# Shift rows transposed in the first place of their slot, and projections read once from the turn bank: four stages of attention on one core

## The chip, the cores and the metric

The kernel runs on one core of a Trainium2 chip. Its time is the device time of one execution in microseconds (us), and of several runs the median counts. The engines are named as in the profile: PE is TensorE's matmuls and PEld its weight loads, DVE is VectorE, ACT is ScalarE, POOL is GpSimd, and SP is SyncE, which issues most DMA transfers. ACTq is ScalarE's own queue of DMA issues.

## What is computed

Sixteen sequences of 512 tokens and 256 features go through four residual layers, each on the layer norm of its input: causal attention, a guided attention that splits the tokens into two classes, rotary attention, and the guided attention again. All have 16 heads of 16 features. From the reference, shortened:

```python
x = x + _L0_attn_a_ref(_layernorm(x), Wq, bq, Wk, bk, Wv, bv, Wo, bo)      # causal
x = x + _L0_ffn_ref(_layernorm(x), g_info, W_qkv, W_proj, b_proj)          # guided
x = x + _L0_attn_b_ref(_layernorm(x), Wqkv, Wo)                            # rotary
x = x + _L0_ffn_ref(_layernorm(x), g_info, W_qkv, W_proj, b_proj)          # guided
...
# guided: the class of a token is its mean cosine with g_info, scaled to 0..1 over all tokens, > 0.9
logits = jnp.einsum('bqhd,bkhd->bhqk', q * scale, k)
l = jnp.where(key_mask[:, None, None, :], logits, -jnp.inf)
a = jax.nn.softmax(l, axis=-1)
```

## The kernel before

**Stages and batches.** The four layers are the stages 0 to 3: `STAGES = [CAUSAL, SPLIT, ROTARY, SPLIT]`. A stage runs over 16 batches, one sequence each. While a batch of a stage is in attention, the batch before it is finished (output projection, residual, layer norm, and the projections q, k and v of the next stage, called `nx`, `nq`, `nv`). In stage 0 the projections of later batches of its own (`xt`, `qk`, `v`) come on top. The classes of a guided stage need all of its tokens, so there is a full stop ahead of stages 1 and 3; stage 2 follows stage 1 without one.

**Precision.** q and k are each split into three bf16 parts (`parts`: high, middle, low), which go out to memory and come back as stacked rows of `q_stack` and `k_stack`, so that one bf16 matmul over 96 to 100 rows gives the exact scores.

**Slots.** A batch has 16 slots. In slot n, TensorE does in this order: four matmuls of `scores_t` (keys on the partitions; L1235), of which ScalarE takes the exponential into `probs` (L1072); score tiles 0 and 1 of the head six slots ahead (L1204), of which VectorE takes the maximum (L874); the turn of the first place; the output sums `o_ps` (L1256); tiles 2 and 3; the turn of the second place. The two banks of the score tiles alternate, so a tile waits for the maximum two tiles back. There are four heads to a group, and a group g starts its `scores_t` in slot 4g.

**The shift.** When the 16 maxima of a group are there, VectorE writes their negative as two bf16 parts into `shift_parts` (a cast, L884, and a subtraction, L886; semaphore `shift_ready`). The turn `sh` transposes them on TensorE (L1302), VectorE copies them to `shift_rows` (L924), and ScalarE's queue issues the transfer into two rows of `q_stack` (L1092). `scores_t` of the group waits for it (`shift_in`). The maxima of groups 1, 2 and 3 are complete at the end of slots 1, 5 and 9, and those of the next batch's group 0 at the end of slot 13.

**Turns.** All small products of a batch share one bank, `turn_ps`. `TURNS_FIRST` (stage 0) and `TURNS_LATER` (the others) say which turns stand in the first and in the second place of a slot; an entry is (kind, which batch, part). Turns whose batch or stage has no use for them drop out: stage 3 has no `nx`, `nq`, `nv`, `sim`, `simt`. A turn on TensorE counts up `turn_full`; whoever takes it out of the bank counts up `turn_free`, and the next turn waits for that. `v`, `sh`, `og`, `xo`, `xs`, `out`, `simt` are taken by VectorE, the others by ScalarE.

**Taking a projection.** For q and k ScalarE reads the bank one to three times: into `qk_f` (float), unless the kind is rotary into `parts` (the bf16 high part), and for the q of a guided stage the square into `q_square` (the tile `x_both`). The last of them frees the bank (L1105 to L1118). GpSimd's `prepare` then makes the other parts: three operations of 2.13 us, L727 to L731, with four more before them for rotary. GpSimd also does the last steps of the layer norm's deviation (L698, L700), between `statistics` and `normalise` of VectorE, which `NXT_STATS_AT` and `NXT_NORMALISE_AT` put behind the maxima of given slots and tiles.

## Time and profile before

| what | us |
|---|---|
| median of 3 runs | 4773.22 |
| lowest and highest | 4757.26, 4778.44 |
| the profiled execution | 4780.01 |
| its span | 4778.2 |
| matmuls busy (PE) | 4387.7 |
| VectorE busy | 3161.1 |
| ScalarE busy | 2505.7 |
| GpSimd busy | 1656.3 |

The span is the time from the first to the last instruction of the profiled execution; the device time has 1.8 us around it. A busy time is the sum of an engine's instructions. Stages 0 to 3 lie at about 90 to 1340, 1385 to 2540, 2540 to 3720 and 3790 to 4778 us of the span.

### The profile page before, as it was taken

To read this page: it belongs to the slowest core of one execution; us is meant where nothing else is said; L and a number is where in the kernel's file an instruction comes from. 1 tells how busy PE (TensorE), PEld (TensorE's weight loads), DVE (VectorE), ACT (ScalarE), POOL (GpSimd) and SP (SyncE) were. 2 spreads that over 40 slices of the span, in tenths; PEclk is the share of its full clock that TensorE was granted. 3 is DMA by queue.
4 is the path that set the end of the run, shared out by engine and by line. 5 is a ranking of instruction groups with operands and counts; after the bars stand their busy time and mean duration, and the time that the engine had idled before them with its cause. 6 is when DMAs were issued, how large, how long until landed. Compare 5 with 4: busy or idle time off the path is not lost.

```text
span 4778.2 us, 70632 instructions
## 1 busy us (share of the span) xinstructions
PE 4387.7 (92%) x26116; PEld 1884.1 (39%) x26116; DVE 3161.1 (66%) x6576; ACT 2505.7 (52%) x3362; POOL 1656.3 (35%) x922
## 2 busy tenths in 40 slices
PE   4999999999969999999999999999999699999999
PEld 2455555555423333333333333333333233333333
DVE  4545555555447677776767777677677288888886
ACT  1454444445425555555555555655655256555555
POOL 2364545555432345353443433433433400000000
PEclk8999999999969999999999999999999799999999
DMA  4453535454322343433424433433433233333331
GB/s 134 126 162 125 161 119 162 135 158 130 116 80 80 100 121 96 119 105 96 130 87 119 124 98 111 124 98 112 124 97 112 74 86 90 92 89 90 90 90 38
DMA packets 302406, 525.36 MB, mean 110 GB/s; under 512 B 58348, under 2 KB 236272, under 8 KB 285680
## 3 DMA queue, kind: packets, MB, share of 16 engines
q1 hardware_dynamic: 259568, 485.19, 34.7%
q10 hardware_dynamic: 42496, 35.66, 2.3%
q8 instruction: 209, 3.42, 0.3%
q14 instruction: 133, 1.09, 0.1%
HBM read 317.10 MB, written 201.46 MB: 109 GB/s over the span
## 4 chain that ended last, share of the span: by engine, by line
PE 70%; DVE 13%; DMA 8%; ACT 4%; issue 4%; POOL 1%; ACTq 0%; SPq 0%; POOLq 0%; DVEq 0%
PE o_ps L1256 15%; PE scores L1204 15%; PE scores_t L1235 11%; PE turn_ps L1284 10%; DVE neg_max L874 9%; DMA q_stack<-shift_rows 8%; PE turn_ps L1331 5%; PE turn_ps L1291 5%; PE turn_ps L1262 4%; PE turn_ps L1296 1%; DVE xn L842 1%; ACT probs L1072 1%; DVE bn L824 1%; PE scores L1207 1%; PE scores_t L1238 1%
## 5 line engine op out<-in xcount | busy, mean ns | idle before, releaser
L874 DVE TENSOR_REDUCE neg_max<-scores 128x1 f32<-128x512 f32 (+3 forms) x4096 | 2457.7, 635 | 1250.0 <-PE scores L1204 750.7
L1072 ACT ACTIVATE probs<-scores_t 128x1024 f32<-128x1024 f32 (+2 forms) x2048 | 1890.4, 946 | 1325.4 <-PE scores_t L1235 924.8
L1204 PE MATMUL scores<-k_stack,q_stack 98*128 98x512 bf16 (+4 forms) x4096 | 1286.5, 370 | 113.6 <-DVE neg_max L874 65.4
L1235 PE MATMUL scores_t<-q_stack,k_stack 100*128 100x512 bf16 (+3 forms) x4096 | 1035.8, 364 | 106.4 <-DMA q_stack<-shift_rows 105.6
L1256 PE MATMUL o_ps<-probs,values 128*32 128x512 f32 (+1 forms) x8192 | 1015.1, 568 | 0.0
L1204 PEld LDWEIGHTS scores<-k_stack,q_stack 96*128 96x128 bf16 (+1 forms) x4096 | 358.0, 97 | 1321.8 <-DVE neg_max L874 930.5
L1235 PEld LDWEIGHTS scores_t<-q_stack,k_stack 100*128 100x128 bf16 x4096 | 373.1, 98 | 536.8 <-DMA q_stack<-shift_rows 145.0
L727 POOL TENSOR_TENSOR parts<-qk_f,parts 128x1024 bf16<-128x1024 f32 x128 | 272.4, 2128 | 558.6 <-ACT parts L1112 394.4
L747 POOL TENSOR_TENSOR sim_inv<-sim_parts,minus_half 128x64 f32<-128x64 f32 x32 | 337.6, 10550 | 235.5 <-DVE sim_parts L956 235.5
L740 POOL TENSOR_TENSOR x_res<-x_res,o_bias_s 128x1024 f32<-128x1024 f32 x32 | 75.8, 2370 | 942.1 <-DMA x_res<-x_after 942.1
L698 POOL TENSOR_SCALAR var_eps<-mean_var 128x4 f32<-128x4 f32 x64 | 14.7, 229 | 971.3 <-DVE mean_var L831 971.3
L1112 ACT ACTIVATE qk_f<-turn_ps 128x512 f32<-128x512 f32 x192 | 114.6, 597 | 337.8 <-PE turn_ps L1284 337.8
L1256 PEld LDWEIGHTS o_ps<-probs,values 128*32 128x32 f32 x8192 | 161.8, 108 | 315.4 <-issue 251.4
L731 POOL TENSOR_TENSOR parts<-rest,parts 128x1024 bf16<-128x1024 f32 x128 | 273.4, 2136 | 10.0
L729 POOL TENSOR_TENSOR rest<-qk_f,parts 128x1024 f32<-128x1024 f32 x128 | 272.6, 2130 | 10.0
L1207 PE MATMUL scores<-causal_qk,ident_b 128*128 128x128 bf16 x1024 | 220.1, 222 | 0.0
L1238 PE MATMUL scores_t<-causal_kq,ident_b 128*128 128x128 bf16 x1024 | 192.6, 220 | 0.0
L715 POOL TENSOR_TENSOR rest<-qk_f,sin_t 128x1024 f32<-128x1024 f32 x32 | 75.7, 2367 | 299.9 <-ACT qk_f L1112 297.6
L1079 ACT COPY out_sums<-o_ps 128x512 f32<-128x512 f32 x256 | 151.4, 591 | 33.9 <-PE o_ps L1256 33.8
L1262 PE MATMUL turn_ps<-ident,out_sums 128*128 128x128 f32 x1024 | 157.9, 277 | 2.1 <-ACT out_sums L1079 2.1
L1284 PE MATMUL turn_ps<-xn_t,wq_split 128*128 128x512 f32 x256 | 134.0, 648 | 15.7 <-ACT x_both L1117 12.0
L947 DVE TENSOR_TENSOR x_res<-turn_ps,x_res 128x512 f32<-128x512 f32 x128 | 88.5, 692 | 79.0 <-PE turn_ps L1331 79.0
(117 smaller groups left out, 4045.4 us busy)
## 6 DMA issues: line engine op xcount, KB each, us to landing
q_stack<-q_parts SPq DMA_DIRECT2D x1536, 64.0 KB, 2.6
values<-v_stage SPq DMA_DIRECT2D x64, 1024.0 KB, 4.0
values<-values SPq DMA_DIRECT2D x64, 1024.0 KB, 6.2
k_parts<-parts SPq DMA_DIRECT2D x192, 256.0 KB, 2.7
q_parts<-parts SPq DMA_DIRECT2D x192, 256.0 KB, 3.8
k_stack<-k_parts SPq DMA_DIRECT2D x256, 192.0 KB, 3.2
k_stack<-k_parts SPq DMA_DIRECT2D x256, 128.0 KB, 3.1
x_after<-x_res ACTq DMA_DIRECT2D x48, 512.0 KB, 3.2
```

The costliest lines, as they stand in the source:

```text
L727: last = nc.gpsimd.tensor_tensor(middle, x, high, ALU.subtract)
L729: last = nc.gpsimd.tensor_tensor(rest[:, :, :], x, high, ALU.subtract)
L731: last = nc.gpsimd.tensor_tensor(low, rest[:, :, :], middle, ALU.subtract)
L747: nc.gpsimd.tensor_tensor(sim_inv[:, :], sim_parts[:, 1, :], minus_half[:, :], ALU.pow).then_inc(sim_pow.sem, 1)
L874: nc.vector.tensor_reduce(neg_max[:, h % G, t:t + 1], bank[:, 0:n], AX.X, ALU.max, negate=True).then_inc(max_done.sem, 1)
L1072: nc.scalar.activation(probs[c][:, h % G, 0:n], st[i][:, 0:n], ACT.Exp).then_inc(exp_done.sem, 1)
L1204: last = nc.tensor.matmul(bank[:, 0:n], q[0:r, h, t * P:(t + 1) * P], k[0:r, h, 0:n], start=True, stop=kind != CAUSAL)
L1207: last = nc.tensor.matmul(bank[:, t * P:(t + 1) * P], ident_b[:, :], causal_qk[:, :], start=False, stop=True)
L1235: last = nc.tensor.matmul(st[i][:, off:off + L - q0], k[0:ROWS, h, kt * P:(kt + 1) * P], q[0:ROWS, h, q0:L], start=True, stop=kind != CAUSAL)
L1256: last = nc.tensor.matmul(o_ps[VW * h:VW * (h + 1), q0:L], values[B.n % 2][:, kt, G * g + h, :], probs[kt // 2][:, h, off:off + L - q0], s ...
L1262: last = nc.tensor.transpose(turn_ps[:, t * P:(t + 1) * P], tile(t), ident[:, :])
L1284: last = nc.tensor.matmul(turn_ps[:, :], weight[:, kt, m * P:(m + 1) * P], xn_t[:, kt, :], start=kt == 0, stop=kt == KT - 1)
```

## The change

It has two parts. First, in slots 2, 6, 10 and 14 the turn `sh` takes the first place and the turn beside it the second; ScalarE issues the transfer of the shift rows at the end of its work on that slot, behind the turn of the second place, instead of in the next slot. Since `out` 1 now ends slot 6, pieces of the statistics that need it move from (6, 3) and (7, 0) to (7, 0) and (7, 1), and the last step from (7, 1) to (7, 2). Second, a projection is read from the bank once, into `qk_f`, and this frees the bank; the copy to `parts` and the square are made from `qk_f`, behind a wait of ScalarE on its own first copy. A new semaphore, `projected`, tells GpSimd and the turn `sim` that they are done.

```diff
 TURNS_FIRST = {
-    2: ([("qk", 2, 0)], [("sh", 0, 1)]),
+    2: ([("sh", 0, 1)], [("qk", 2, 0)]),
...
 TURNS_LATER = {
-    2: ([], [("sh", 0, 1)]),
+    2: ([("sh", 0, 1)], []),
...
-    6: ([("out", -1, 1)], [("sh", 0, 2)]),
+    6: ([("sh", 0, 2)], [("out", -1, 1)]),
...
-    10: ([("nq", -1, 2)], [("sh", 0, 3)]),
+    10: ([("sh", 0, 3)], [("nq", -1, 2)]),
...
-    14: ([("nv", -1, 1)], [("sh", 1, 0)]),
+    14: ([("sh", 1, 0)], [("nv", -1, 1)]),
...
-NXT_STATS_AT = {(6, 0): 0, (6, 2): 1, (6, 3): 2, (7, 0): 3, (7, 1): T}
+NXT_STATS_AT = {(6, 0): 0, (6, 2): 1, (7, 0): 2, (7, 1): 3, (7, 2): T}
...
+        def is_projected(s, n, k):
+
+            return k == "qk" or (k == "nq" and next_split(Batch(s, n).s))
+
+        projected = Count(sem("projected"), steps_of(
...
-                turn_free.wait(pool, B, FRONT[f][1], a + 1)
+                if kind_of(B, f) == ROTARY:
+                    turn_free.wait(pool, B, FRONT[f][1], a + 1)
+                else:
+                    projected.wait(pool, B, FRONT[f][1], a + 1)
...
-                        project = lambda dst: nc.scalar.activation(dst, turn_ps[:, :], ACT.Identity, bias=bias, scale=scale)
+                        nc.scalar.activation(qk_f[:, i, :], turn_ps[:, :], ACT.Identity, bias=bias,
+                                             scale=scale).then_inc(turn_free.sem, 1)
                     else:
-                        project = lambda dst: nc.scalar.activation(dst, turn_ps[:, :], ACT.Copy, scale=scale)
-                    last = project(qk_f[:, i, :])
+                        nc.scalar.activation(qk_f[:, i, :], turn_ps[:, :], ACT.Copy, scale=scale).then_inc(turn_free.sem, 1)
                     if kind != ROTARY:
-                        last = project(parts[:, i, 0, :])
-                    if kind == SPLIT and i < 2:
-                        last = nc.scalar.activation(q_square[:, i, :], turn_ps[:, :], ACT.Square, scale=scale)
-                    last.then_inc(turn_free.sem, 1)
+
+                        act.wait_ge(turn_free.sem, turn_free.after(B, k, i))
+                        last = nc.scalar.copy(parts[:, i, 0, :], qk_f[:, i, :])
+                        if kind == SPLIT and i < 2:
+                            last = nc.scalar.activation(q_square[:, i, :], qk_f[:, i, :], ACT.Square)
+                        last.then_inc(projected.sem, 1)
...
-                        if not place:
-
-                            for k, o, i in turns_of(B.s, B.n, slot - 1, 1):
+                        if place:
+                            for k, o, i in turns_of(B.s, B.n, slot, 0):
                                 if k == "sh":
                                     shift_dma(B + o, i)
...
+                elif k == "sim":
+                    pe.wait_ge(projected.sem, projected.after(B, "nq", 1))
```

TensorE, stage 2, the end of slot 13 (`sim`, its last row) to the start of slot 15. Before:

```order
L1297 MATMUL turn_ps<-x_both,head_sel 32x512
L1235 MATMUL scores_t<-q_stack,k_stack 128x512 x4
L1204 MATMUL scores<-k_stack,q_stack 128x512 x2
L1291 MATMUL turn_ps<-wv_split,xn_t 128x256 x4
L1256 MATMUL o_ps<-probs,values 32x512 x4
L1204 MATMUL scores<-k_stack,q_stack 128x512 x2
L1302 MATMUL turn_ps<-ident_b,shift_parts 32x128
L1235 MATMUL scores_t<-q_stack,k_stack 128x512 x4
```

The same place of the change (its lines are numbered 13 to 15 higher):

```order
L1312 MATMUL turn_ps<-x_both,head_sel 32x512
L1248 MATMUL scores_t<-q_stack,k_stack 128x512 x4
L1217 MATMUL scores<-k_stack,q_stack 128x512 x2
L1317 MATMUL turn_ps<-ident_b,shift_parts 32x128
L1269 MATMUL o_ps<-probs,values 32x512 x4
L1217 MATMUL scores<-k_stack,q_stack 128x512 x2
L1306 MATMUL turn_ps<-wv_split,xn_t 128x256 x4
L1248 MATMUL scores_t<-q_stack,k_stack 128x512 x4
```

The transpose of `shift_parts` and the projection `nv` have changed places; the transpose now stands right behind tiles 0 and 1, and the output sums and tiles 2 and 3 stand behind it.

ScalarE, stage 2, slots 12 (the second `nq` turn) to 15, with what each row waits for. Before:

```order
L1112 ACTIVATE qk_f<-turn_ps 128x512 [waits q_parts_out,prep,turn_full]
L1112 ACTIVATE parts<-turn_ps 128x512
L1117 ACTIVATE x_both<-turn_ps 128x512
...
L1123 COPY v_stage<-turn_ps 128x16x16 [waits v_out,turn_full]
L1123 COPY v_stage<-turn_ps 128x16x16
L1072 ACTIVATE probs<-scores_t 128x1024 [waits scores_t_full] x2
L1092 DMA q_stack<-shift_rows 2x16x128 [waits turn_free]
L1072 ACTIVATE probs<-scores_t 128x1024 [waits scores_t_full]
```

The same place of the change:

```order
L1125 ACTIVATE qk_f<-turn_ps 128x512 [waits q_parts_out,prep,turn_full]
L1129 CAST parts<-qk_f 128x512 [waits turn_free]
L1131 ACTIVATE x_both<-qk_f 128x512
...
L1137 COPY v_stage<-turn_ps 128x16x16 [waits v_out,turn_full]
L1137 COPY v_stage<-turn_ps 128x16x16
L1104 DMA q_stack<-shift_rows 2x16x128 [waits turn_free]
L1084 ACTIVATE probs<-scores_t 128x1024 [waits scores_t_full] x2
```

The second and third copy read `qk_f`, the second behind a wait. The issue of the transfer has moved ahead of two exponentials, and stands right behind the two copies of `nv`.

VectorE, stage 2, from the add of `out` in slot 6 to the first `xn` in slot 8. Before:

```order
L947 TENSOR_TENSOR x_res<-turn_ps,x_res 128x512
L874 TENSOR_REDUCE neg_max<-scores 128x1
L824 BN_STATS bn<-x_res 128x6
L874 TENSOR_REDUCE neg_max<-scores 128x1
L924 COPY shift_rows<-turn_ps 32x128
L824 BN_STATS bn<-x_res 128x6
...
L831 BN_AGGR mean_var<-bn 128x2 x4
L874 TENSOR_REDUCE neg_max<-scores 128x1 x3
L842 TENSOR_SCALAR xn<-x_res,mean_var,rstd 128x256
```

The same place of the change, from the copy of `shift_rows`:

```order
L936 COPY shift_rows<-turn_ps 32x128
L886 TENSOR_REDUCE neg_max<-scores 128x1
L836 BN_STATS bn<-x_res 128x6
L886 TENSOR_REDUCE neg_max<-scores 128x1
L959 TENSOR_TENSOR x_res<-turn_ps,x_res 128x512
...
L843 BN_AGGR mean_var<-bn 128x2 x4
L886 TENSOR_REDUCE neg_max<-scores 128x1 x2
L854 TENSOR_SCALAR xn<-x_res,mean_var,rstd 128x256
```

The copy now comes ahead of the last two maxima of slot 6, the add of `out` behind them, and between `mean_var` and the first `xn` there are two maxima instead of three.

## Rows read from the trace of the kernel before

**Rows 1.** The page, busy time and share of the span of each engine.

```profile
PE 4387.7 (92%) x26116; PEld 1884.1 (39%) x26116; DVE 3161.1 (66%) x6576; ACT 2505.7 (52%) x3362; POOL 1656.3 (35%) x922
```

**Rows 2.** Waits in stages 0, 1, 2, 3: us in total, times, longest.

```profile
PE scores_t L1235 <- DMA q_stack<-shift_rows: 27.1, 22, 2.5
...
PE scores_t L1235 <- DMA q_stack<-shift_rows: 37.2, 28, 2.8
...
PE scores_t L1235 <- DMA q_stack<-shift_rows: 21.8, 25, 2.1
...
PE scores_t L1235 <- DMA q_stack<-shift_rows: 19.4, 22, 1.4
```

**Rows 3.** Groups of instructions: count | busy us, mean ns | idle before, its causes.

```profile
L1284 PE MATMUL turn_ps<-xn_t,wq_split 128*128 128x512 f32 x256 | 134.0, 648 | 15.7 <-ACT x_both L1117 12.0 <-ACT xn_t L1098 1.3 <-ACT parts L1112 0.5
...
L1284 PE MATMUL turn_ps<-xn_t,wk_causal 128*128 128x512 f32 x256 | 129.0, 627 | 10.1 <-ACT parts L1110 8.7 <-ACT xn_t L1098 1.4
L1291 PE MATMUL turn_ps<-wv_split,xn_t 128*128 128x256 f32 x512 | 125.3, 387 | 15.7 <-ACT x_both L1117 11.9 <-ACT parts L1112 2.4 <-ACT v_stage L1123 1.5
...
L1284 PE MATMUL turn_ps<-xn_t,wq_causal 128*128 128x512 f32 x256 | 123.0, 602 | 12.4 <-ACT parts L1110 12.4
...
L884 DVE CAST shift_parts<-neg_max 128x16 bf16<-128x16 f32 x256 | 109.9, 429 | 8.9
```

**Rows 4.** Timeline, stage 1, slots 14 and 15: start, duration, [idle before].

```profile
1963.30 2.13 POOL L729 TENSOR_TENSOR rest<-qk_f,parts 128x1024 f32<-128x1024 f32 x1
...
1963.80 1.67 DVE L884 CAST shift_parts<-neg_max 128x16 bf16<-128x16 f32 x1
...
1964.05 1.89 PE L1291 MATMUL turn_ps<-wv_causal,xn_t 128*128 128x256 f32 x8
1965.50 0.18 DVE L886 TENSOR_TENSOR shift_parts<-neg_max,shift_parts 128x16 bf16<-128x16 f32 x1
...
1967.40 0.23 PE L1302 MATMUL turn_ps<-ident_b,shift_parts 128*32 128x128 bf16 x1
...
1968.73 0.62 ACTq L1092 DMA_DIRECT2D q_stack<-shift_rows  x1
...
1973.07 1.04 PE L1235 MATMUL scores_t<-q_stack,k_stack 100*128 100x512 bf16 x4 [2.07 <-DMA q_stack<-shift_rows]
```

**Rows 5.** Timeline, stage 2, slot 13.

```profile
3066.85 1.99 PE L1291 MATMUL turn_ps<-wv_split,xn_t 128*128 128x256 f32 x8 [0.37 <-ACT x_both L1117]
3066.88 2.13 POOL L727 TENSOR_TENSOR parts<-qk_f,parts 128x1024 bf16<-128x1024 f32 x1 [0.76 <-ACT x_both L1117]
...
3068.88 0.65 ACT L1123 COPY v_stage<-turn_ps 128x256 f32<-128x256 f32 x2 [1.17 <-PE turn_ps L1291]
...
3071.29 2.13 POOL L731 TENSOR_TENSOR parts<-rest,parts 128x1024 bf16<-128x1024 f32 x1
3071.53 1.92 DVE L884 CAST shift_parts<-neg_max 128x16 bf16<-128x16 f32 x1
```

**Rows 6.** Timeline, stage 3, slot 14 to the next batch's slot 0.

```profile
4221.35 0.17 DVE L886 TENSOR_TENSOR shift_parts<-neg_max,shift_parts 128x16 bf16<-128x16 f32 x1
...
4221.49 1.06 PE L1256 MATMUL o_ps<-probs,values 128*32 128x512 f32 x8
4221.56 2.64 DVE L874 TENSOR_REDUCE neg_max<-scores 128x1 f32<-128x512 f32 x4
...
4224.35 0.62 ACTq L1092 DMA_DIRECT2D q_stack<-shift_rows  x1
...
4227.93 1.04 PE L1235 MATMUL scores_t<-q_stack,k_stack 100*128 100x512 bf16 x4 [1.10 <-DMA q_stack<-shift_rows]
```

**Rows 7.** Timeline, stage 2, slot 7: mean_var, rstd and xn.

```profile
3040.49 0.37 DVE L831 BATCH_NORM_AGGREGATE mean_var<-bn 128x2 f32<-128x6 f32 x4
...
3041.26 1.04 POOL L700 TENSOR_TENSOR rstd<-var_eps,minus_half 128x4 f32<-128x4 f32 x1
...
3042.55 0.41 DVE L842 TENSOR_SCALAR xn<-x_res,mean_var,rstd 128x256 f32<-128x256 f32 x1
```

More of the change, by code:

```diff
@@ L90 @@
     5: ([("ex", 0, 0)], [("out", -1, 0)]),
-    6: ([("out", -1, 1)], [("sh", 0, 2)]),
+    6: ([("sh", 0, 2)], [("out", -1, 1)]),
     7: ([("og", 0, 0)], [("xo", 0, 0)]),
     9: ([("nx", -1, 0)], [("nx", -1, 1)]),
-    10: ([("nq", -1, 2)], [("sh", 0, 3)]),
+    10: ([("sh", 0, 3)], [("nq", -1, 2)]),
     11: ([("og", 0, 1)], [("nq", -1, 3)]),
@@ L97 @@
     13: ([("nv", -1, 0)], [("sim", -1, 0)]),
-    14: ([("nv", -1, 1)], [("sh", 1, 0)]),
+    14: ([("sh", 1, 0)], [("nv", -1, 1)]),
     15: ([("og", 0, 2)], [("simt", -1, 0)]),
 }
-NXT_STATS_AT = {(6, 0): 0, (6, 2): 1, (6, 3): 2, (7, 0): 3, (7, 1): T}
+NXT_STATS_AT = {(6, 0): 0, (6, 2): 1, (7, 0): 2, (7, 1): 3, (7, 2): T}
 NXT_NORMALISE_AT = {(8, t): t for t in range(T)}
@@ L388, in hybrid_blocks @@
         turn_free = Count(sem("turn_free"), steps_of(*turn_args))
+        def is_projected(s, n, k):
+            return k == "qk" or (k == "nq" and next_split(Batch(s, n).s))
+        projected = Count(sem("projected"), steps_of(
+            lambda s, b: [t for t in turn_steps(s, b) if is_projected(s, b + t[0], t[1][0])],
+            lambda s: [t for t in turn_args[1](s) if is_projected(s, t[0], t[1][0])],
+            lambda s: [t for t in finish_turns(s) if is_projected(s, NB - 1, t[0])]))
         def max_steps(s, b):
```

## The prediction

> **What bounds the kernel now.** I read the page first, then the waits by stage, the groups by line, and last the timeline of one batch in each of stages 1, 2 and 3. On the page TensorE is busy 92% of the span, VectorE 66%, ScalarE 52%, GpSimd 35% [rows 1]. So TensorE's row is nearly full, and a change pays only where it removes a gap from that row, or costs where it puts one in. The waits by stage show the biggest kind of gap: TensorE stands at the first `scores_t` tile of a head group until the shift rows have landed in `q_stack`, 27.1 + 37.2 + 21.8 + 19.4 = 105.5 us over the four stages, in 22 + 28 + 25 + 22 = 97 waits [rows 2]. The second kind is at the turn bank: the next turn waits until ScalarE has made all two or three copies of a projection. The matmul idle before the projections names it as 12.0 + 0.5, 8.7, 12.4 and 11.9 + 2.4 us, 47.9 us together [rows 3]. These two are what the change works on. A third thing is to be seen in the same view: the cast into `shift_parts` on VectorE has a mean of 429 ns [rows 3], while the subtraction behind it, of the same shape, takes 0.17 us when nothing disturbs it [rows 6]. What the cast takes beyond that is the subject of the third term.
>
> **Term A, the transfer of the shift rows goes out earlier.** Before, the transpose is the last work of slots 2, 6, 10 and 14, so the transfer leaves early in the next slot. In stage 3 it is issued at 4224.35, and the tile that needs it starts at 4227.93, 3.58 us later, after 1.10 us of idle TensorE [rows 6]. The transpose could have begun once `shift_parts` was there, at 4221.35 + 0.17 = 4221.52, when TensorE began the output sums (4221.49). After the change VectorE still does two maxima first (2.64 us for four, so 1.32) and the copy of 0.2 us, so the issue falls near 4223.1, some 1.2 us earlier [rows 6]. That covers the 1.10 us. Stage 3 has no projections that come between: of its 19.4 us I take 18.
> In stages 0 to 2 ScalarE takes the other turn of the slot first if it is one of its own: `nq` in slot 10, `nv` in slot 14, and `qk` in slot 2 of stage 0. That turn now ends the slot, so in slot 14 the issue is not early: it waits for `nv`. What is left is small. Before, in stage 1, the transpose closed the slot at 1967.40 + 0.23 and the issue came at 1968.73, 1.1 us later, after a maximum and the copy on VectorE [rows 4]. Now the issue has only `nv`'s two copies of `v_stage` ahead of it, and needs no more than the start of the second: the two take 0.65 us and start 0.04 us behind the matmuls (3066.85 + 1.99 against 3068.88 [rows 5]), so it comes some 0.4 to 0.5 us behind the slot's end. The gain is 0.4 us in stage 0 and 0.6 in stages 1 and 2 per batch, or 6.5 + 9 + 10 us for 15, 15 and 16 batches. The rest of the waits of these stages lies at slots 4 and 8, whose transposes are in slots 2 and 6, beside `out` (a VectorE turn) or nothing. With the mean wait of a stage (37.2 / 28 = 1.33 and 21.8 / 25 = 0.87 us [rows 2]) for the fifteen or sixteen waits at slot 0, slots 4 and 8 hold 37.2 - 20 = 17 us in stage 1 and 21.8 - 14 = 8 us in stage 2. There the issue comes 1 to 3 us earlier: I take 8, and 12 of the 17, since VectorE is late in slots 8 and 9 too and would hold the next tiles. Stage 0 keeps its slot 4, where `qk` stands before the transfer. A = -(18 + 12 + 9 + 8 + 10 + 6.5) = -63.5 us. Ends: nothing to -105.5.
>
> **Term B, one read of the bank.** The bank is released after the first copy, so 0.60 us (one copy less) or 1.2 us (two less) earlier. Each wait shown is shorter than this: 0.37 us before `nv` in stage 2, for one [rows 5]. Nothing but the first copy stands between the matmuls and the release, so these gaps close; of the 47.9 us I take 44, since `sim` and the preparation still wait for all copies. B = -44. Ends: 0 (the time is given back at the next wait) to -48. ScalarE does as many operations as before, plus one wait on itself each; at 52% [rows 1] it hides that, and the causal copies lose their bias.
> The copies now read SBUF. The Trainium skill (VectorE: DVE Perf Modes, "The TRN2 errata") has ScalarE's SBUF-to-SBUF operation 52 cycles dearer than from PSUM, which speaks against the change: an estimate of 0.04 us for each of 256 copies, 11 us on ScalarE. The sum would be the same by it while ScalarE has idle time; the trace of before has no such copy of this size.
>
> **Term C, a new wait.** The transpose now stands right behind tile 1 of its slot, and everything on TensorE queues behind it: the output sums, tiles 2 and 3, the other turn. It waits for `shift_parts`, which before was covered by a turn and the sums. In stage 1 GpSimd's subtraction starts at 1963.30 and takes 2.13; the cast starts at 1963.80 and takes 1.67, so it ends with it, at 1965.47, and `shift_parts` is there at 1965.68 [rows 4]. TensorE was at the place of the transpose at 1964.05: 1.6 us of new idle. GpSimd's rotary preparation is in the same phase in nearly every batch of the stage, and nothing in the change moves it there: 15 x 1.6 = 24 us.
> The Trainium skill says the same of the mechanism (SBUF — State Buffer, "SBUF: two separate sides"): VectorE and GpSimd share a pair of SBUF ports that one instruction holds to its end. By that rule the cast waits out GpSimd's operation whole; the trace agrees, with 1.67 us for an operation of a size that takes 0.17, and the sum is the same.
> In stage 2 the cast falls 0.24 us behind the start of a GpSimd operation and takes 1.92 us (3071.29, 3071.53 [rows 5]). Term B takes 0.4 to 0.5 us out of slot 13 ahead of it, while GpSimd's start (3066.88 less the wait for the copies) moves little against the matmuls. The cast then meets the end of the operation before, and ends two microseconds earlier: no new wait. If the phase stays, it costs 16 x 0.6 = 10 us. Where nothing collides, `shift_parts` comes 0.1 to 0.2 us behind TensorE's arrival (4221.52 against 4221.49, and the semaphore [rows 6]): some 30 slots of stage 3, 16 of stage 2, 15 of stage 0 with 0.3, together 9 + 3 + 4 us. Slot 2 of stage 1 has collisions as well, but there VectorE holds tile 2 anyway: 4; first batches 2. C = 24 + 9 + 3 + 4 + 4 + 2 = +46. Ends: 15 (no collision) to 150 (below).
>
> **Term D, the statistics.** `out` 1 now ends slot 6, so the statistics of the next layer norm move into slot 7, and the last step from after maximum (7, 1) to after (7, 2). Before, `mean_var` was done by 3040.86, GpSimd had `rstd` at 3041.26 + 1.04 = 3042.30, and VectorE wanted it at 3042.55, with three maxima between [rows 7]. With two there, VectorE comes 0.6 us sooner and waits up to 0.35, and it has one more `bn_stats` (0.3 to 0.4 us) in its full stretch. In stage 2 that is 0.7 x 15 = 10 us; in stage 1 `xo` gives `rstd` its time, 5 us; in stage 0 the causal maxima are shorter, nothing. D = +15. Ends 0 to 30.
>
> Swapping which pair of tiles has the long turn behind it costs nothing: the short side is the sums (1.06 us) instead of `scores_t` (1.04) [rows 6], and both cover one maximum and most of the second. TensorE's instructions stay the same, and nothing in the change touches its clock.
>
> **Sum.** -63.5 - 44 + 46 + 15 = -46.5 us on the profiled execution of 4780.0 us, so 4733.5. That execution is 0.14% above the median of the runs shown (4773.2), so 4727 for the median.
>
> **Rivals.**
> 1. *B is given back.* VectorE or the transfer ends the next wait and TensorE only arrives there earlier. For it: TensorE's tiles alternate with VectorE's maxima in every slot. Against: slots 12 and 13, where most of these waits sit, hold projection turns of 1.99 us [rows 5], in which VectorE catches up. -46.5 + 44 = -2.5: 4771.
> 2. *The transfer is not earlier* except in stage 3, because ScalarE reaches the issue only after its two exponentials and a wait for the copy. A shrinks to -18, the sum to -1: 4772. Against: ScalarE is idle nearly half the span [rows 1].
> 3. *More comes off.* The collision of stage 1 gives way and the waits at slot 0 go too: A = -105, C = 22: -105 - 44 + 22 + 15 = -112: 4661.
> 4. *Slower.* The new wait meets a GpSimd operation in slots 14 and 2 of all of stages 0 to 2. Each collision costs 1.6 us on TensorE. The forecast has 15; 29 more eat the gain (46.5 / 1.6), 44 more make it slower by over 0.5%. With 64 more: -46.5 + 102 = +56: 4829. For it: GpSimd's preparations run in these slots, one after another. Against: in stage 2 slot 14 `shift_parts` came when TensorE arrived, and the mean cast of 429 ns [rows 3] leaves only 256 x 0.25 = 65 us of blocking in all.
>
> **How the numbers follow.** Chances: forecast 0.53, rival 1 0.19, rival 2 0.06, rival 3 0.13, rival 4 0.09. The forecast's own range is 4695 to 4755. Rivals 1 and 2 lie near 4772, so the range for 8 in 10 is 4680 to 4774: it takes in half of rival 3 and leaves rival 4 out. A measurement of this kernel tells about 0.5%, 24 us, from no change. Faster by more: nearly all of the forecast and rival 3, 0.66. Within: 0.25. Slower: 0.09.
>
> **What would show it.** A: the waits of `scores_t` for the shift rows fall from 105.5 to about 40 us, nearly all at slot 0 of stages 0 to 2, and to under 2 us in stage 3. B: no matmul waits for `parts` or `x_both`. C: a new group, the transpose waiting for `shift_parts`, 35 to 50 us, most of it in stage 1 slot 14. D: `xn` waits for `rstd`, 5 us in stage 2. The prediction is wrong if C is above 90 us, if stage 3 is not shorter by 10 us (it has A and hardly anything else), or if stage 1 gains more than stage 2.

## The result and the profile after

The change takes 4613.5 us (median of 4 runs, 4608.4 to 4615.5); the kernel before took 4775.8 on the same chip. The ratio is 0.9652, with a 95% interval of 0.9598 to 0.9705. A second comparison on another chip gave 0.958 (0.956 to 0.9601). Medians of the kernel before range from 4776 to 4814 us from chip to chip, so experiments are compared by ratio. I had said 4727, a gain of 46.5 us; the gain is 162. The direction was right, the size was not.

The page after, busy time of each engine and the chain that ended last:

```profile
PE 4319.8 (94%) x26116; PEld 1910.3 (41%) x26116; DVE 3158.6 (68%) x6576; ACT 2501.0 (54%) x3362; POOL 1657.0 (36%) x922
...
PE 77%; DVE 17%; issue 3%; POOL 1%; ACT 1%; DMA 1%; POOLq 0%; DVEq 0%; SPq 0%; ACTq 0%
```

The span is 4613.3 us against 4778.2. TensorE's share rose from 92% [rows 1] to 94%, with the same 26116 matmuls. In the chain, DMA had 8% before and has 1% now.

The waits of TensorE for the two things that term A and term C speak of, in stages 0, 1, 2 and 3 of the change (us in total, times, longest):

```profile
PE scores_t L1248 <- DMA q_stack<-shift_rows: 0.6, 1, 0.6
PE turn_ps L1317 <- DVE shift_parts L898: 0.2, 1, 0.2
...
PE turn_ps L1317 <- DVE shift_parts L898: 46.1, 29, 2.1
...
PE turn_ps L1317 <- DVE shift_parts L898: 6.1, 4, 3.5
PE scores_t L1248 <- DMA q_stack<-shift_rows: 0.2, 1, 0.2
...
PE turn_ps L1317 <- DVE shift_parts L898: 3.8, 4, 1.4
```

Against [rows 2], 105.5 us of waits for the shift rows are gone, also those of slot 0, of which I had kept most. The new wait for `shift_parts` is 56.2 us in all, and 46.1 of it is in stage 1. The groups that answer to [rows 3]:

```profile
L1299 PE MATMUL turn_ps<-xn_t,wk_causal 128*128 128x512 f32 x256 | 131.2, 637 | 3.2 <-ACT qk_f L1122 1.8 <-ACT xn_t L1110 1.4
L1299 PE MATMUL turn_ps<-xn_t,wq_split 128*128 128x512 f32 x256 | 128.0, 623 | 2.8 <-ACT qk_f L1125 1.4 <-ACT xn_t L1110 1.4
L1299 PE MATMUL turn_ps<-xn_t,wq_causal 128*128 128x512 f32 x256 | 125.8, 614 | 3.1 <-ACT qk_f L1122 3.1
L1306 PE MATMUL turn_ps<-wv_split,xn_t 128*128 128x256 f32 x512 | 123.2, 383 | 2.8 <-ACT v_stage L1137 1.5 <-ACT qk_f L1125 1.4
L1129 ACT CAST parts<-qk_f 128x512 bf16<-128x512 f32 x192 | 118.7, 618 | 6.0
L896 DVE CAST shift_parts<-neg_max 128x16 bf16<-128x16 f32 x256 | 98.9, 386 | 8.8
```

No projection waits for `parts` or `x_both` any more: 15.7 + 10.1 + 12.4 + 15.7 = 53.9 us of idle time have become 11.9.

Where the time went by stage, from the start of `scores_t` of a stage's first slot to that of its last slot, read from the timelines:

| stage | before, from, to | after, from, to | length |
|---|---|---|---|
| 0 | 111.1, 1309.4 | 112.4, 1222.4 | 1198.3 to 1110.0, -88 |
| 1 | 1397.4, 2570.9 | 1307.9, 2470.9 | 1173.5 to 1163.0, -10 |
| 2 | 2576.4, 3719.4 | 2474.2, 3578.5 | 1142.9 to 1104.4, -39 |
| 3 | 3807.0, 4757.2 | 3662.2, 4591.6 | 950.2 to 929.4, -21 |

Stage 1 gained least. Its slot 14, timeline of the change (start, duration, [idle before]), beside [rows 4]:

```profile
1874.45 2.12 POOL L741 TENSOR_TENSOR rest<-qk_f,parts 128x1024 f32<-128x1024 f32 x1
...
1874.92 1.69 DVE L896 CAST shift_parts<-neg_max 128x16 bf16<-128x16 f32 x1
1876.64 0.18 DVE L898 TENSOR_TENSOR shift_parts<-neg_max,shift_parts 128x16 bf16<-128x16 f32 x1
...
1876.87 0.23 PE L1317 MATMUL turn_ps<-ident_b,shift_parts 128*32 128x128 bf16 x1 [1.54 <-DVE shift_parts L898]
...
1880.35 0.37 ACT L1137 COPY v_stage<-turn_ps 128x256 f32<-128x256 f32 x1 [4.17 <-PE turn_ps L1306]
1880.36 0.62 ACTq L1104 DMA_DIRECT2D q_stack<-shift_rows  x1
...
1881.02 0.33 SPq L632 DMA_DIRECT2D values<-v_stage  x1
...
1883.42 1.03 PE L1248 MATMUL scores_t<-q_stack,k_stack 100*128 100x512 bf16 x4
```

The first half is term C as forecast: the cast ends with GpSimd's operation and TensorE stands for 1.54 us. The second half is what I had not seen. The transfer is issued 0.01 us behind the start of the *first* copy of `v_stage`, and the store of `values` by SyncE follows 0.66 us later. In stage 2 of the kernel before, the order was the other one:

```profile
3076.06 0.34 SPq L623 DMA_DIRECT2D values<-v_stage  x1
3076.44 2.78 SPq L618 DMA_DIRECT2D q_parts<-parts  x3
...
3078.15 0.62 ACTq L1092 DMA_DIRECT2D q_stack<-shift_rows  x1
...
3081.74 1.04 PE L1235 MATMUL scores_t<-q_stack,k_stack 100*128 100x512 bf16 x4 [0.85 <-DMA q_stack<-shift_rows]
```

The DMA view of that stretch (queue: packets, MB, share of 16 engines; q10 is ScalarE's queue, q1 SyncE's), first 3078.15 to 3080.90, where it has no row for q10, then 3080.90 to 3081.74:

```profile
q1 hardware_dynamic: 567, 1.01, 100.6%
...
q1 hardware_dynamic: 247, 0.24, 94.4%
q10 hardware_dynamic: 34, 0.01, 4.3%
```

For 2.75 us after its issue none of the transfer's 34 packets moved. The store was not alone in front: its last packet started at 3079.34, and from there to 3081.00 the packets of SyncE's queue were the smaller ones of other transfers, of `q_parts` (256 KB each) among them. In the change all 34 are through 1.65 us after the issue (2960.95 to 2962.60, the same place in stage 2):

```profile
q1 hardware_dynamic: 16, 0.13, 19.2%
q10 hardware_dynamic: 34, 0.01, 2.2%
```

In stage 1 of the kernel before, the order is different again. Beside the transfer of [rows 4], issued from 1968.73 for 0.62 us, SyncE has:

```profile
1967.69 1.42 SPq L618 DMA_DIRECT2D k_parts<-parts  x3
1969.16 0.49 SPq L623 DMA_DIRECT2D values<-v_stage  x1
```

Here the issue of the store ends 0.3 us behind that of the transfer, as in 14 of the 15 batches of this stage with both (1.6 us in the other), and what stands in front is `k_parts`. The first of the 34 packets moved 2.16 us after the issue, the last 3.95 us after it, between packets of the store.

So a theory to test, for stages 0 and 2 first: **a transfer of 8 KB lands in some 1.5 us when it is ahead of the 1 MB store, and in 3 us and more behind it, and the gain at slot 0 hangs on that order.** The rival: it is only the earlier issue that counts.

### The profile page after: what moved, and what is told of

Its sections match the earlier page's. It is cut to its first block, busy times and chain, and to the rows that moved or that the text cites. A ratio compares the mean times of both kernels' runs of the same rounds, so it can differ in the third digit from the quotient of the medians.

```text
span 4613.3 us, 70664 instructions
## 1 busy us (share of the span) xinstructions
PE 4319.8 (94%) x26116; PEld 1910.3 (41%) x26116; DVE 3158.6 (68%) x6576; ACT 2501.0 (54%) x3362; POOL 1657.0 (36%) x922
## 4 chain that ended last, share of the span: by engine, by line
PE 77%; DVE 17%; issue 3%; POOL 1%; ACT 1%; DMA 1%; POOLq 0%; DVEq 0%; SPq 0%; ACTq 0%
PE o_ps L1269 18%; PE scores L1217 17%; DVE neg_max L886 11%; PE scores_t L1248 11%; PE turn_ps L1299 10%; PE turn_ps L1275 6%; PE turn_ps L1346 5%; PE turn_ps L1306 5%; PE turn_ps L1311 1%; DVE xn L854 1%; PE scores L1220 1%; PE scores_t L1251 1%; PE turn_ps L1317 1%; DVE bn L836 1%; DVE shift_parts L896 1%
## 5 line engine op out<-in xcount | busy, mean ns | idle before, releaser
L1084 ACT ACTIVATE probs<-scores_t 128x1024 f32<-128x1024 f32 (+2 forms) x2048 | 1850.9, 943 | 1129.3 <-PE scores_t L1248 879.1
L1248 PEld LDWEIGHTS scores_t<-q_stack,k_stack 100*128 100x128 bf16 x4096 | 393.9, 98 | 441.2 <-issue 119.3
L1137 ACT COPY v_stage<-turn_ps 128x256 f32<-128x256 f32 x192 | 62.1, 375 | 197.1 <-PE turn_ps L1306 197.1
```

What stands on the lines that cost most here:

```text
L1084: nc.scalar.activation(probs[c][:, h % G, 0:n], st[i][:, 0:n], ACT.Exp).then_inc(exp_done.sem, 1)
L1248: last = nc.tensor.matmul(st[i][:, off:off + L - q0], k[0:ROWS, h, kt * P:(kt + 1) * P], q[0:ROWS, h, q0:L], start=True, stop=kind != CAUSAL)
```

## The experiments

**1. The two parts apart.** `p1_only` is the change with the old copies from the bank (the old lines L1105 to L1118); `p2_only` is the kernel before with the new ones.

```diff
 # p2_only, against the change
-    14: ([("sh", 1, 0)], [("nv", -1, 1)]),
+    14: ([("nv", -1, 1)], [("sh", 1, 0)]),
... (and slots 2, 6, 10, NXT_STATS_AT and the place of shift_dma)
```

Expected of the first: 

> The swap of the turns with the early issue and the moved statistics, and the three copies read from the bank as before the change. Measured so far: the change is 164.9 us of span shorter. Theory (waits for the transfer carry most of it): the matmul waits for the shift rows are gone here too, the waits for parts and x_both stay; 65 to 110 us shorter than before, near 4680. Rival (the release of the bank carries most of it, since TensorE's rows hide 0.16 us of each wait): 40 us shorter, near 4735.

Expected of the second: 

> The copies made from qk_f with the bank released after the first, and nothing else changed. Theory: 60 to 75 us shorter than before, from slots 1, 2, 12 and 13 of stage 0 and slots 12 and 13 of stage 2, near 4710; waits for the shift rows unchanged at about 105 us. Rival (the two parts help each other, and alone the freed time ends in the wait for the transfer at slot 0 or 4): under 40 us, with waits for the shift rows above 120.

Measured: `p1_only` 0.9796 (0.976 to 0.9831), 4705.3 against 4803.6 us; `p2_only` 0.983 (0.9784 to 0.9875), 4716.9. Their product is 0.963, against 0.965 and 0.958 for the change, so they add up to it as far as can be told. I had given the first part -2.5 us; it is worth 98. The second, at -44, came out at 87 by the medians (60 to 104 by the interval) and at 51 in the profiled spans (4727.3). The waits for the shift rows with the second part alone:

```profile
PE scores_t L1249 <- DMA q_stack<-shift_rows: 111.3, 98, 5.5
```

They are as long as in [rows 2]: the copies do nothing for them. By stage `p2_only` is 45 and 17 us shorter in stages 0 and 2 and 3 us longer in stage 3, but 17 us longer in stage 1, where the waits at slot 8 grew from 12.0 to 20.6 us and TensorE spent more time at the lower clock (7 below).

**2. The issue later, two ways.** `issue_next` issues in the next slot behind its first exponential; `issue_done` keeps the place, but ScalarE first waits until its two copies of `v_stage` are complete.

```diff
 # issue_next
-                        if place:
-                            for k, o, i in turns_of(B.s, B.n, slot, 0):
+                        if not place:
+                            for k, o, i in turns_of(B.s, B.n, slot - 1, 0):
 # issue_done, behind "if k == "sh":"
+                                    for k2, o2, i2 in turns_of(B.s, B.n, slot, 1):
+                                        if k2 not in DVE_TURNS:
+                                            act.wait_ge(turn_free.sem, turn_free.after(B + o2, k2, i2))
```

Expected of `issue_next`: 

> The changed kernel with the transfer of the shift rows issued in the next slot behind the first exponential, where it stood before the change. Theory 1 (only the moment of issue matters): it is issued 0.6 us behind the slot's end instead of 0 to 0.2, so a wait of 0.8 us comes back at slot 0 of all stages and part of those at slots 4 and 8: 60 to 90 us longer than the change, near 4690. Theory 2 (the transfer also lands sooner because the store of the values is now issued behind it): waits of 0.3 to 0.5 us at slot 0 of stages 0 to 2, 20 to 40 us longer, near 4645.

Expected of `issue_done`: 

> The changed kernel with one wait added: where ScalarE takes the second turn of the slot (nv, nq, and qk in stage 0), the transfer is issued only when that turn's copies are complete, 0.65 us later than in the change. Theory 1 (moment of issue): slots 0 to 2 of the stages see waits of 0.7 to 1 us at slot 0, 35 to 50 us longer than the change. Theory 2 (order against the store of the values): the store waits for the same copies and is issued at the same moment, so the landing is late by the queueing as well, up to 60 us longer. Rival (there is slack of over 0.65 us): no difference.

Measured: 0.9778 (0.9748 to 0.9808) and 0.9765 (0.9723 to 0.9806). Of the change's gain (0.9652 and 0.958 in its two comparisons) between a third and a half is lost either way. In `issue_done` the transfer is issued only 0.67 us later than in the change (456.17 against 455.50 in stage 0), and TensorE waits 1.60 us at the next batch, where the change has no wait:

```profile
456.17 0.33 SPq L632 DMA_DIRECT2D values<-v_stage  x1
456.17 0.65 ACTq L1104 DMA_DIRECT2D q_stack<-shift_rows  x1
...
460.35 0.39 PE L1251 MATMUL scores_t<-q_stack,k_stack 100*128 100x512 bf16 x1 [1.60 <-DMA q_stack<-shift_rows]
```

The DMA view of `issue_done`, 456.17 to 459.50, then 459.50 to 460.35:

```profile
q1 hardware_dynamic: 128, 1.05, 77.8%
...
q1 hardware_dynamic: 270, 0.25, 88.7%
q10 hardware_dynamic: 34, 0.01, 4.3%
```

All 128 packets of the store go first; the 34 of the transfer follow from 459.59 to 459.94, mixed with those of `q_parts`. Both were issued at the same moment, but SyncE's issue takes 0.33 us and ScalarE's 0.65. `issue_next` shows how sharp the edge is. In stage 1:

```profile
1894.99 0.62 ACTq L1104 DMA_DIRECT2D q_stack<-shift_rows  x1
1895.22 0.33 SPq L632 DMA_DIRECT2D values<-v_stage  x1
...
1899.27 1.04 PE L1248 MATMUL scores_t<-q_stack,k_stack 100*128 100x512 bf16 x4 [1.48 <-DMA q_stack<-shift_rows]
```

ScalarE's issue began first, but ended at 1895.61, SyncE's at 1895.55; TensorE waits 1.48 us. Six of the 34 packets moved before the store was through, the first at 1897.62. In stage 0 of the same kernel ScalarE's issue runs from 453.54 for 0.65 us and SyncE's from 453.92 for 0.33, so ScalarE's ends first, at 454.19 against 454.25, and there is no wait. Over the whole kernel it is the same: in the 14 batches of stage 0 with a store beside the transfer ScalarE's issue ends 0.07 to 0.09 us ahead and TensorE doesn't wait at slot 0; ahead of the 30 waits at slot 0 of stages 1 and 2 (41.3 us) it ends 0.05 to 0.08 us behind. By stage, `issue_next` is 5, 37, 28 and 1 us longer than the change (starts in the timelines, as in the table above). The total fits the rival's figure (4693 against 4690), but the rival, that only the time of issue counts, put the waits at slot 0 of all stages, and they are 2.0 and 0.0 us in stages 0 and 3 and 22.5 and 18.8 in stages 1 and 2. It falls, as the only cause. Up to 17 of the 37 us of stage 1 can be the clock (7 below).

**3. The store held back, in the kernel before.** The whole edit:

```diff
                     store_parts(before, NXT, "k")
+                    if there(B.s, B.n + 1):
+                        shift_in.wait(sp, B + 1, 0)
                     store_values(before, NXT)
```

> The kernel before the change with one wait added on SyncE's queue: the store of the values of nv (1 MB) goes out only when the shift rows of the next batch's group 0 have landed. The transfer of the shift rows is issued at the same moment as before. Theory (the store in front of it is what makes it land late, 2.8 to 3.2 us to its last packet against 1.5 alone): the waits at slot 0 of stages 1 and 2 fall from about 1.1 us to under 0.3, and those of stage 0 too, 30 to 50 us shorter than before; stage 3, which has no such store, unchanged. Rival (the landing takes what it takes, only the moment of issue counts): the same waits, time unchanged or longer by what the held loads cost.

Measured: 0.9798 (0.9775 to 0.9821), 4704.0 against 4800.4 us. One wait on SyncE, with the old order of turns and the old place of the issue, gives 96 us by the medians (67 in the profiled spans), as much as the whole first part of the change. SyncE issues in order, so the wait holds back also what it issues behind the store, `q_parts` and the next loads; no run holds the store alone. The waits for the shift rows:

```profile
PE scores_t L1237 <- DMA q_stack<-shift_rows: 59.1, 67, 5.0
```

They fell from 105.5 to 59.1. At slot 0 they went from 17.8 to 2.2 us in stage 0, from 14.2 to 1.1 in stage 2, and only from 16.6 to 8.8 in stage 1, where `k_parts` still stands in front; the 16.2 left at slot 0 of stage 3, which has no store, are untouched by it. By stage it took 21, 47, 2 and -5 us. The 47 of stage 1 include 33 in slots 2, 3 and 7, far from slot 0. The waits for the shift rows at slots 4 and 8, which count in slots 3 and 7, fell by 17 us, and up to 12 us can be the clock (7 below); why these waits fell no run separates.

**4. GpSimd out of the way.** `short_prep` is the change, with the rotary preparation on GpSimd made on 8 of 512 columns. It leaves out the rest of those parts of q and k in stage 2.

```diff
+                if kind_of(B, f) == ROTARY:
+                    N = 8
+                    x, high, middle, low = (v[:, :, 0:N] for v in (x, high, middle, low))
```

> The changed kernel with GpSimd's preparation of the rotary q and k cut to 8 of 512 columns, so those parts are left as they were; all waits and transfers stay. Theory (the new wait of the transpose in stage 1 is VectorE's cast or subtraction held up by GpSimd's operation): slot 14 of stage 1 falls from 7.1 us back to about 5.5, slot 2 by 0.4, the cast's mean in that slot from 1.57 to 0.17 us, 25 to 35 us shorter than the change. Rival (the wait is the swap's own cost): slot 14 stays above 6.5.

Measured: 0.9466 (0.9448 to 0.9484), 4545.8 us on the chip of `hold_store`; stage 1 is 60 us shorter than in the change. TensorE's wait in stage 1:

```profile
PE turn_ps L1323 <- DVE shift_parts L904: 2.1, 1, 2.1
```

From 46.1 us to 2.1: the wait is GpSimd's doing. The slots give 32 us at slot 14 and 26 at slot 2, where I had put 4; the profiled span is 62 us shorter than in the change, about twice the 25 to 35 expected. Up to 17 of it can be the clock (7 below).

**5. The change again, and three variants beside it on one chip.** `keep14` takes slot 14 of stage 1 in its old order, `stats_old` puts the statistics back, `issue_early` issues the transfer ahead of the turn of the second place.

```diff
 # keep14
+    if s == 1 and slot == 14:
+        first, second = second, first
 # stats_old
-NXT_STATS_AT = {(6, 0): 0, (6, 2): 1, (7, 0): 2, (7, 1): 3, (7, 2): T}
+NXT_STATS_AT = {(6, 0): 0, (6, 2): 1, (6, 3): 2, (7, 0): 3, (7, 1): T}
```

The change: 

> The changed kernel itself, as the reference for the kernels sent with it: a ratio of 0.965 to before, as measured.

`keep14`: 

> The changed kernel with slot 14 of stage 1 alone as before the change: nv in the first place, the transpose last, the transfer issued in slot 15. The wait for shift_parts there (1.65 us in 14 batches) is covered again, but the transfer is issued late and behind the store of the values. Theory: slot 14 falls from 7.1 to 5.1 us and slot 15 rises from 3.3 to 4.5, 8 to 14 us shorter than the change. Rival: the landing behind the store takes 4.3 us as in the run that issued it late, slot 15 rises to 5, and the time is the same.

`stats_old`: 

> The changed kernel with the statistics of the next layer norm back at (6, 3), (7, 0) and (7, 1), which VectorE's order still allows. Theory (the moved statistics cost a wait for rstd and crowd slot 7): the 13.5 us of waits for rstd go, slot 8 of stage 2 falls by 0.6 us, 5 to 12 us shorter than the change. Rival: VectorE is late in slot 7 either way, no difference.

`issue_early`: 

> The changed kernel with the transfer of the shift rows issued ahead of ScalarE's second turn of the slot, right after the second exponential, so up to 3 us earlier in slots 10 and 14, and 2 of stage 0. Theory (no wait for it is left, 0.7 us in all): no difference, within 0.3%. Rival (ScalarE then stands waiting for VectorE's copy and takes nq and nv later, or the landing still has a hidden part): 10 us either way.

Measured: 0.958 (0.956 to 0.9601), 0.9574 (0.9553 to 0.9595), 0.9568 (0.9548 to 0.9589) and 0.9575 (0.9555 to 0.9595). The intervals overlap, so the three variants can't be told from the change by their times. The traces tell more. In `keep14` the slot 14 is 34 us shorter over stage 1 than in the change beside it and slot 15 is 25 longer; there the issue stands in slot 15, behind other transfers:

```profile
1872.30 1.42 SPq L629 DMA_DIRECT2D k_parts<-parts  x3
...
1873.34 0.64 ACTq L1106 DMA_DIRECT2D q_stack<-shift_rows  x1
1873.76 0.50 SPq L634 DMA_DIRECT2D values<-v_stage  x1
...
1877.35 1.45 PE L1254 MATMUL scores_t<-q_stack,k_stack 100*128 100x512 bf16 x4 [1.74 <-DMA q_stack<-shift_rows]
```

ScalarE's issue ended at 1873.98, ahead of the store's 1874.26 but behind that of three transfers of `k_parts`, 256 KB each (1873.72). The tile waited, for a transfer issued 4.0 us before. So it isn't the store alone that can stand in front, and the kernel before has this order in stage 1 throughout. In `stats_old` slot 8 of stage 2 is 11 us shorter, and the waits of the layer norm in the whole kernel go from the first row (the change) to the second:

```profile
DVE xn L854 <- POOL rstd L709: 13.5, 23, 1.5
```

```profile
DVE xn L854 <- POOL rstd L709: 9.0, 5, 2.3
```

`issue_early` brings nothing: the transfer was ahead of the store already.

**6. What the findings give together.** `best` is the change with `keep14`, `stats_old` and `hold_store`. `hold_p2` is the kernel before with `hold_store` and the copies, without the swap of turns.

`best`: 

> Three edits on the change: slot 14 of stage 1 in its former turn order (its transfer issued in slot 15), the statistics slots as in the kernel before, and SyncE waits for the next batch's shift rows before it issues the store of values. Theory (the length of a landing is set by the store that stands ahead of it in the queues, so the wait of the first slot of a batch in stage 1 goes once the store is held back): stage 1 shows no gap at either slot 14 or slot 15, beyond the 1 us by which the issue is later, and the three gains add: from 4614.5 about 9 for the statistics, 9 + 20 in stage 1, so 4575 to 4595, ratio 0.952 +- 0.003. Rival (the landing of that slot is long because it is issued late, whatever else is in the queues): slot 15 keeps its 4.5 us, the sum is keep14 and stats_old alone, 4600, ratio 0.9555. A second rival: the held store comes late for those who read the values, and the time rises above 4610.

`hold_p2`: 

> The kernel before with the copies part of the change and the one wait on SyncE that keeps the store of values behind the shift transfer; its order of turns is the old one. It asks what the changed order of turns is worth beyond putting the transfer ahead of the store. Theory (most of the first part's gain at the batch's start is the store): the two gains multiply, 0.983 x 0.98 = 0.963, about 4625 to 4640 where before is 4805, and the remainder to the change's 0.958 (20 to 25 us) is the landing's own 1.1 us that the earlier issue still saves at the batch's start, less the wait in slot 14. Rival (the earlier issue counts for more: other slots of the batch lose their waits by it as well): the ratio stays at 0.970 or above. Second rival (the two overlap in the same waits for the copies): 0.975.

Measured: `best` 4555.0 against 4793.6 us, 0.9496 (0.9461 to 0.953); `hold_p2` 4640.0, 0.9671 (0.9631 to 0.971). The waits of `best`:

```profile
PE turn_ps L1325 <- DVE shift_parts L902: 10.6, 20, 1.8
PE scores_t L1256 <- DMA q_stack<-shift_rows: 10.1, 17, 0.7
```

Its stage 1 is 48 us shorter than in the change: 31 at slot 14, 19 at slot 2 and 5 each at slots 0 and 3, less 12 at slot 15. The tile of slot 0, which waited 1.74 us in `keep14`, waits 0.58. The `k_parts` stand in front of both; the store, issued 0.3 us behind the transfer in `keep14`, still mixed its packets with it there (the last of the 34 started 3.64 us after the issue, in `best` 2.48). The ratio is what was expected (0.952 +- 0.003), the median 20 us better than its range. The interval of `hold_p2` (0.9631 to 0.971) decides nothing between the theory (0.963) and the first rival (0.970 and up). What the swap adds once SyncE is held is seen better against `best`, on the same chip: `best` has the swap everywhere but in slot 14 of stage 1, and is 85 us faster by the medians, 30, 12, 32 and 29 us by stage. So the earlier issue counts too, also where no store is near: `hold_p2` keeps 21.5 us of waits in stage 3, `best` none. The plain change is 35 us shorter than `hold_p2` in the profiled spans, where I had given 20 to 25. By stage the change is 30, -36, 18 and 26 us shorter than `hold_p2`: the swap pays in stages 0, 2 and 3, and costs 36 us in stage 1, to slots 14 and 2; up to 17 of these can be the clock.

**7. TensorE's clock in stage 1.** The experiments differ in one more thing. Between the full stops TensorE's granted clock is at its upper level (2.4 GHz) nearly throughout stages 0, 2 and 3, but in stage 1 it falls to the lower one (1.2 GHz) for short stretches, in the change mostly in slots 14 and 2. In one slot 14 of the change, with the view of the windows behind it (busy time by engine, then the granted clock):

```profile
2022.38 0.23 PE L1317 MATMUL turn_ps<-ident_b,shift_parts 128*32 128x128 bf16 x1 [1.50 <-DVE shift_parts L898]
2022.48 1.69 PE L1269 MATMUL o_ps<-probs,values 128*32 128x512 f32 x8
```

```profile
2019.40:2022.40 3.00, 1.41 (x7) 0.41 (x5) 2.90 (x5) 2.32 (x3) 2.84 (x3) 1.00 0.00 0
2022.80:2025.80 3.00, 3.00 (x13) 1.16 (x6) 2.02 (x5) 0.00 (x0) 2.86 (x2) 0.50 0.21 69
```

TensorE had stood 1.50 us, and the output sums behind it took 1.69 us instead of 1.06. From the second batch of stage 1 to its last slot, the time at the lower level is 31 us in the kernel before, 34 in the change, 31 in `p1_only`, 51 in `p2_only`, 68 in `issue_next`, 61 in `issue_done`, 27 in `keep14`, 7 in `hold_store`, and none in `short_prep`, `best` and `hold_p2`. At half the clock at most half of such time is lost, so by this estimate the difference between two kernels has up to half of the difference of these figures in it: next to nothing between before and after, up to 17 us where the change is set against `issue_next`, `short_prep`, `best` or `hold_p2`, up to 12 for `hold_store` against before. No run separates it from the waits that it follows.

## Why the prediction was off

The rest of this section counts by slot: the mean time from one slot's first tile to the next one's, in `p1_only` and `p2_only` against before, times 16.

**Term A (-63.5): the step that failed.** In `p1_only` the slots ahead of a group's first tile (3, 7, 11, 15) lost 112 us, more than my outer end of 105.5. I had written for stages 0 to 2 that the issue in slot 14 "is not early: it waits for `nv`" and took 25.5 us there for 0.4 to 0.6 us per batch. Slot 15 lost 22, 21 and 16 us, 59 in these three stages. Two things were missing. The issue needs the start of the first copy of `v_stage`, not of the second, 0.3 us. And I took the landing as a constant, though my own rows show 3.58 us in one place [rows 6] and the wait of 2.07 after an issue at 1968.73 means 4.34 in another [rows 4]. I asked how much earlier the transfer leaves and never what stands in front of it: the store and `q_parts` in stages 0 and 2, `k_parts` in stage 1. Experiments 2 and 3 show it from both sides: behind the store the wait of 1.5 us is back, and holding SyncE back removes it in stages 0 and 2 and halves it in stage 1. Stage 3, which has no `nv` and no store, gained more than the 18 - 9 = 9 us of A and C: the 19.4 us of waits of [rows 2] are gone, and the stage is 21 us shorter. In `p1_only` its slots ahead of a first tile lost 13 us, and slots 2, 6, 10 and 14, to which C gave 9 more, lost 15; this second part stays open.

The Trainium skill has a rule that I should have weighed (DMA: Bandwidth & Descriptors, "Issuing engines are not separate DMA queues"): DMAs started by different engines run on the same 16 engines and interleave. The trace agrees that they share, with 0 of 34 packets moved in 2.75 us. It agrees that they interleave behind the store of `issue_done`, where the 34 packets moved among those of `q_parts`, but not with the store itself, whose 128 all went first. "Queues, rings and completion order" on the same page has an engine alternate between queues after a whole packet, typically of 9 to 17 descriptors. The store's 128 are 8 for each of 16 engines, so this would fit if the 8 made up one such packet; whether they did, no run here shows.

**Term C (+46): the mechanism right, the sum too large.** Stage 1 slot 14 was put at 24 us; the wait there is 22.9 us, and the slot grew by 28 in `p1_only` and 31 in the change. Stage 2 had no new wait, as guessed. The small waits "where nothing collides" (9 + 3 + 4 us) are not there: 3.8, 6.1 and 0.2 us in the rows above, and slots 2, 6, 10 and 14 together grew by only 7 us. Slots 6 and 10 lost 14; I had put the exchange of the long and the short side at nothing, and no run separates this. Slot 2 of stage 1 was put at 4 us; its wait is 23.3 us, half of the 46.1, and it is worth 19 to 26 (`best`, `short_prep`), though the slot is only 6 us longer than before. So the waits came out at 56 us, above the 46; what was too large is what they cost net, and no run says where the rest came back.

**Term D (+15)**: `stats_old` gives 9 us by the medians, 12 in stage 2 of the trace.

**Term B (-44)**: 51 in the profiled spans, 87 by the medians, so mis-sized by 7 or more. The idle rows count too little. Where nothing holds it, a matmul row starts before the modelled end of the one ahead: 2959.01 + 1.89 = 2960.90 for the projection in slot 14 of stage 2 of the change, and the next `scores_t` starts at 2960.74. A gap begins to show as idle only after these 0.16 us, so 97 waits are 15 us longer than their rows say, and shorter ones show nothing. For the whole change the rows of idle time account for (4778.2 - 4387.7) - (4613.3 - 4319.8) = 97 us of 165; the other 68 are in TensorE's busy time, with the same matmuls. The 0.16 us explain only a small part of these: TensorE's idle stretches went from 801 to 763, which is 6 us. The rest is not separated. For the copies the Trainium skill's 52 cycles from SBUF (VectorE: DVE Perf Modes, "The TRN2 errata") had given an estimate of 0.04 us each; the trace has 618 ns against 592 from the bank before, 0.03. It cost nothing that shows.

**The rivals.** In the change nothing shows as given back (1), though `p2_only`, which gained 62 us in stages 0 and 2, was 17 us longer in stage 1; the transfer was earlier (2); and the new wait stayed in stage 1 (4). Rival 3, "more comes off", named the slot 0 waits, but by no mechanism, and bounded its gain by the idle rows. The waits of `scores_t` were to fall to about 40 us, and fell to 0.8: this sign spoke against term A. The signs named for the prediction being wrong (C above 90 us, stage 3 not shorter by 10, stage 1 gaining more than stage 2) did not appear, so they could not catch this error.

So of the 96 us by which the first part was off, 48 are term A, 39 term C and 6 term D (-112, +7, +9, and +3 elsewhere, against -63.5, +46, +15); the rest is the difference between one profiled pair and the medians.

## What to carry to other kernels

A wait for a small transfer has two parts, when it leaves and what is in the queues ahead of it. Look at the large transfers that another engine issues within a few microseconds, and keep the small urgent one ahead by a wait on the issuer of the large one: here one such wait was worth 2%, as much as the first part of the change. It does not replace the earlier issue: with SyncE held, the swap was worth another 85 us. Measure a gap on TensorE by the starts of its neighbours, not by the idle row, and before you put a matmul directly behind a small VectorE operation, look at what GpSimd does at that moment.

## What was new about the hardware

- An 8 KB transfer on ScalarE's queue: all 34 packets through 1.65 us after the issue with nothing ahead, none moved in the first 3.3 us behind a 1 MB store on SyncE's queue (`issue_done`, 128 packets first). A store issued 0.3 us behind it still delayed it where `k_parts` stood ahead: the last packet started 3.64 us after the issue (`keep14`), with the store held 2.48 us (`best`).
- Which of two queues was served first went with the end of the issue, not with its start (or, which is the same here, ScalarE's had to start more than about 0.3 us ahead): with ends at 454.19 (small) and 454.25 (store) the tile had no wait, with 1895.61 and 1895.55 it waited 1.48 us, with 456.82 and 456.50 1.60 us.
- ScalarE's queue issued a DMA before the operation ahead of it ended: 0.01 us after the start of a copy of 0.37 us in the change (1880.35 and 1880.36), and 0.53 us after the start of an exponential of 1.02 us in the kernel before (3077.62 and 3078.15).
- A cast into `shift_parts` that met a GpSimd operation took 1.69 us (1874.92); the shortest and the median of all 256 are 0.17.
- From the second batch of stage 1 of the change on, TensorE's granted clock fell to 0.50 ten times, each time in a slot 14 or 2 and behind a wait for `shift_parts` of 1.44 to 2.07 us; behind 19 other such waits of 1.42 to 2.06 us there it did not fall. At one of the ten eight matmuls of the output sums took 1.69 us instead of 1.06.
